# Maxima of the scores as quads beside the wide products, and unit sums shared between POOL and VectorE

## What is computed

```
def _qdq(x):                       # int8 fake quantisation of the last axis
    s = jnp.maximum(jnp.max(jnp.abs(x), axis=-1, keepdims=True) / 127.0, 1e-08)
    return jnp.clip(jnp.round(x / s), -127.0, 127.0) * s
# attention; x here is layernorm(x)
q = _qdq(x) @ _qdq(wq).T + bq
kv = cond @ wkv.T + bkv
attn = jax.nn.softmax(jnp.einsum('bnhd,bmhd->bhnm', q, k) * scale, axis=-1)
o = jnp.einsum('bhnm,bmhd->bnhd', attn, v).reshape(B, N, C)
out = _qdq(o) @ _qdq(wp).T + bp
# layer
x = x + tanh(g_xattn) * attention(layernorm(x), ctx)
h = layernorm(x)
x = x + tanh(g_ffn) * ((silu((h @ f8(gate_w)) * gate_scale) * ((h @ f8(up_w)) * up_scale)) @ f8(down_w)) * down_scale
```

## Time and profile before

| | us |
|---|---|
| median of 3 runs | 1103.12 (1101.31 to 1110.62) |
| the profiled execution, its own time | 1105.23 |
| its span, first to last instruction | 1103.5 |
| TensorE busy | 967.0 (88%) |
| VectorE busy | 706.6 (64%) |
| POOL busy | 457.2 (41%) |
| ScalarE busy | 446.8 (40%) |
| mean granted TensorE clock | 0.957 of full speed |

### The profile page before, as it was taken

The page is one execution under the profiler, slowest core; times in us unless marked ns, Lnnn a source line. Parts: engine busy times, 40 slices in busy tenths (PEclk is TensorE's granted clock), DMA queues, the critical chain, the costliest instruction groups (busy, mean ns, idle before and its releaser), DMA issues.

```text
span 1103.5 us, 15274 instructions
## 1 busy us (share of the span) xinstructions
PE 967.0 (88%) x5192; PEld 328.0 (30%) x5192; DVE 706.6 (64%) x985; ACT 446.8 (40%) x793; POOL 457.2 (41%) x416
## 2 busy tenths in 40 slices
PE   4476899998999899988999789989899979985698
PEld 1231111234443212224443212214443312212343
DVE  6879899447638756468557757665666856654522
ACT  4330365642340266662341156673232146674130
POOL 3335788860410288940220088860130066630130
PEclk9698799999999999999999989999999989997799
DMA  7244242220002412010001322001001231000001
GB/s 257 72 117 112 58 120 70 75 87 1 1 18 62 111 55 52 13 57 1 1 7 39 105 79 63 20 20 39 1 1 43 72 91 44 1 1 0 1 1 39
DMA packets 34289, 55.41 MB, mean 50 GB/s; under 512 B 8416, under 2 KB 14624, under 8 KB 34208
## 3 DMA queue, kind: packets, MB, share of 16 engines
q1 hardware_dynamic: 29280, 38.58, 12.1%
q0 software_dynamic: 4800, 15.73, 4.9%
q10 hardware_dynamic: 128, 0.07, 0.0%
HBM read 31.21 MB, written 4.19 MB: 32 GB/s over the span
## 4 chain that ended last, share of the span: by engine, by line
issue 34%; PE 33%; POOL 14%; DVE 11%; ACT 4%; DMA 3%; POOLq 0%; ACTq 0%; DVEq 0%
PE ps L1095 10%; PE ps L1159 7%; PE ps L1148 6%; PE ps L1173 4%; PE ps L1135 3%; POOL acc L498 2%; ACT r L680 2%; DVE mx L906 2%; POOL r L569 2%; PE ps L1386 2%; POOL ctx_hi L469 2%; POOL ctx_lo L473 1%; DMA cf<-in_ctxT 1%; POOL w_down L501 1%; POOL w_up L501 1%
## 5 line engine op out<-in xcount | busy, mean ns | idle before, releaser
L906 DVE TENSOR_REDUCE mx<-ps 128x2 f32<-128x1024 f32 x256 | 306.9, 1220 | 113.5 <-PE ps L1135 107.0
L680 ACT ACTIVATE r<-ps 128x512 f32<-128x512 f32 x512 | 279.7, 595 | 208.3 <-PE ps L1148 189.7
L1148 PE MATMUL ps<-qst,kst 97*128 97x512 f16 x512 | 168.9, 394 | 35.5 <-ACT r L680 25.3
L552 POOL TENSOR_TENSOR acc<-r,acc 128x512 f32<-128x512 f32 x108 | 134.5, 1280 | 16.1 <-ACT r L680 15.3
L1159 PE MATMUL ps<-r,vv 128*32 128x512 f32 x1024 | 140.3, 621 | 0.0
L1135 PE MATMUL ps<-k_reg,q_reg 32*128 32x512 f16 x512 | 102.8, 401 | 17.0 <-DVE mx L906 16.7
L569 POOL TENSOR_TENSOR r<-q_reg,r 128x512 f16<-128x512 f32 x48 | 57.0, 1188 | 142.2 <-ACT r L705 142.2
L522 POOL TENSOR_TENSOR xres<-xres,bp_bc 128x512 f32<-128x512 f32 x16 | 19.7, 1267 | 193.4 <-DMA xres<-in_x 193.3
L1095 PE MATMUL ps<-k_reg,w_gate 128*128 128x512 f16 x384 | 90.7, 379 | 7.2 <-DVE k_reg L1021 7.2
L1031 DVE SCALAR_TENSOR_TENSOR q_reg<-ps,us_c,q_reg 128x512 f32<-128x512 f32 x48 | 35.9, 749 | 88.4 <-PE ps L1095 87.9
L1095 PE MATMUL ps<-k_reg,w_up 128*128 128x512 f16 x384 | 90.7, 379 | 0.0
(11 more groups left out here) (139 smaller groups left out, 1226.0 us busy)
## 6 DMA issues: line engine op xcount, KB each, us to landing
kst<-k_reg SPq DMA_DIRECT2D x192, 64.0 KB, 2.0
qst<-q_reg SPq DMA_DIRECT2D x192, 32.0 KB, 1.9
cf<-in_ctxT POOLq DMA_DIRECT2D x24, 256.0 KB, 3.4
qst<-in_x SPq DMA_DIRECT2D x4, 1024.0 KB, 5.1
xres<-in_x SPq DMA_DIRECT2D x4, 1024.0 KB, 6.2
acc<-in_gate_w POOLq DMA_DIRECT2D x12, 256.0 KB, 3.3
acc<-in_up_w POOLq DMA_DIRECT2D x12, 256.0 KB, 3.0
acc<-in_down_w POOLq DMA_DIRECT2D x12, 256.0 KB, 2.9
```

What stands on the lines that cost most here:

```text
L552: nc.gpsimd.tensor_tensor(acc[:, j, :], prob[:, i % P_SLOTS, :], other, ALU.add).then_inc(p_pool, 1)
L680: nc.scalar.activation(prob[:, i % P_SLOTS, :], bank(S_RING[i % 2]), ACT.Exp, scale=SCALE).then_inc(exp_done, 1)
L906: nc.vector.tensor_reduce(mx[:, g % 2, t, half, 2 * pair:2 * pair + 2], ps[:, M_PAIRS[p % 2]:M_PAIRS[p % 2] + 2, :], AX.X, ALU.max).then_i ...
L1148: nc.tensor.matmul(bank(S_RING[i % 2]), kst[0:97, SLOTS[g], j, t * P:(t + 1) * P], qst[0:97, SLOTS[g], j, :], start=True, stop=True).then_ ...
```

## The change

All four batches are written out in Python; no hardware loop is left. The parts:

- **Order between units.** SX and XT of the next batch stand in the chain ahead of X2T; then come, as one run of wide products `WIDE`, Q0 to Q3, K0 to K7, GU0 to GU23, DOWN0 to DOWN3, in banks 0 to 3 by turns. x of the next batch is normalised and quantised by VectorE during the units (`x_ahead`, at `AHEAD_UNITS`) and not during the gates.
- **Maxima as quads.** A quad computes all four heads of a group at once, in banks 4 to 7, and VectorE reduces it in two instructions of 128x1024. 24 quads (groups 0 to 2) stand between or inside the wide products: one in each of K2 to K7, one behind each gate (a shift step takes one place), two in each DOWN. Group 3's 16 pairs stay in the units, one to a unit, in banks 6 and 7 alone.
- **Batch 0** has group 0 and half of group 1 as quads beside V and ahead of the units, the rest as pairs, two steps at the end of each of units 0 to 20, all in banks 6 and 7.
- **Units.** Two heads' scores go to banks 0, 1, two to banks 2, 3; one exponential takes two banks (128x1024). `values` and `sums` follow the four scores. Sums have bank 5, values bank 4.
- **Additions.** For batches 1 to 3, units 0 to 5 of every group are added: heads 0 and 1 by POOL, heads 2 and 3 by VectorE. Units 6 and 7 stay with TensorE.
- **POOL.** The context of batch b + 2 is split during the gates (three chunks) and DOWN (five) of batch b, and not during units. The residual's bias follows the additions.
- **SP.** k and q are stacked in two slots instead of three. The shift row moves from ScalarE's queue to SP's, behind the group's 24 DMAs. The output is stored by tile in every batch.
- **Memory.** x, its integers, o's transposes and others have tiles of their own or other ones to share.

```diff
-A_RING = (0, 1, 7, 6)
-S_RING = (0, 1)
-M_PAIRS = (2, 4)
-O_BANK, DEN_BANK = 6, 7
+FREE_RING, HEAD_RING, V_RING = (0, 1, 2, 3), (0, 1, 4, 5), (0, 1)
+O_BANK, DEN_BANK, QUAD, PAIR = 4, 5, 4, 6
...
+CHAIN = (["V0"] + CHAIN_LAST[0:5] + ["V1", "V2", "V3"] + CHAIN_LAST[5:9] + ["V4"] + CHAIN_LAST[9:13]
+         + ["V5", "V6", "V7"] + TURNED + CHAIN_LAST[13:])
+WIDE = HI_SEQ + FFN_SEQ
...
+STEPS0 = {"V2": quads(0, 0, 1), "V3": quads(0, 1, 2), "V4": quads(0, 2, 3), "V5": quads(0, 3, 4),
+          "V6": quads(0, 4, 6), "V7": quads(0, 6, 8)}
+LEAD0 = quads(1, 0, 1) + [("S", 0, 0)] + quads(1, 1, 4)
+UNIT_LIST0 = (pairs(1, 8) + pairs(2, 0, 1) + [("S", 1, 0)] + pairs(2, 1) + pairs(3, 0, 1) + [("S", 2, 0)]
+              + pairs(3, 1) + [("S", 3, 0)])
+UNIT_STEPS0 = {u: UNIT_LIST0[2 * u:2 * u + 2] for u in range(G * MT)}
+K_STEPS = {f"K{n}": [s] for n, s in zip(range(2, 8), quads(0, 0, 6))}
+GU_LIST = quads(0, 6, 8) + quads(1, 0, 1) + [("S", 0, 0)] + quads(1, 1) + quads(2, 0, 1)
+DOWN_LIST = [("S", 1, 0)] + quads(2, 1)
+UNIT_STEPS = {u: [s] for u, s in enumerate([("S", 2, 0)] + pairs(3), 1)}
+AHEAD_UNITS = ((2, 4, 6) + tuple(range(16, 32)), (2, 3, 4) + tuple(range(9, 24)))
...
-ADDED, ADDED_LAST = (0, 2, 4, 6), (0, 1, 2, 3, 4, 5)
+ADDED = (0, 1, 2, 3, 4, 5)
+CHUNKS_BY_GATES = (3, 6, 9)
...
 POOL
+                    for j in range(2):
+                        i = u * HG + j
+                        pool.wait_ge(exp_done, pair_count(b, u, j))
...
+                        nc.gpsimd.tensor_tensor(acc[:, j, :], prob[:, i % P_SLOTS, :], other,
+                                                ALU.add).then_inc(p_pool, 1)
...
 ScalarE
+                    for j in range(0, HG, 2):
+                        if u >= 2 and added(b, u - 2):
+                            act.wait_ge(p_pool if j == 0 else p_dve, adds_count(b, u - 2, j + 1))
+                        s = (u * HG + j) % P_SLOTS
+                        act.wait_ge(s_full, pair_count(b, u, j))
+                        nc.scalar.activation(prob[:, s:s + 2, :], ps[:, j:j + 2, :], ACT.Exp,
+                                             scale=SCALE).then_inc(exp_done, 1)
...
 VectorE
+                    if kind == "Q":
+                        t, half = divmod(i, 2)
+                        for k in range(2):
+                            nc.vector.tensor_reduce(mx[:, g % 2, t, half, 2 * k:2 * k + 2],
+                                                    ps[:, QUAD + 2 * k:QUAD + 2 * k + 2, :], AX.X,
+                                                    ALU.max).then_inc(m_free, 1)
...
+                    maxima(b, (UNIT_STEPS if b else UNIT_STEPS0).get(u, []))
+                    if not last and u in AHEAD_UNITS[b > 0]:
+                        next(ahead, None)
+                    if added(b, u):
...
+                        for j in range(2, HG):
...
+                                nc.vector.tensor_tensor(acc[:, j, :], acc[:, j, :], prob[:, i % P_SLOTS, :],
+                                                        ALU.add).then_inc(p_dve, 1)
...
 TensorE
+            def maxima(b, s):
+                kind, g, i = s
+                before = PREVIOUS[b, s]
...
+                else:
+                    pe.wait_ge(m_free, FREE_BEFORE[b, s])
...
+                if kind == "Q":
+                    t, half = divmod(i, 2)
+                    heads, first_bank = range(HG), QUAD
+                else:
+                    t, half, k = i // 4, i // 2 % 2, i % 2
+                    heads, first_bank = range(2 * k, 2 * k + 2), PAIR
+                for k, j in enumerate(heads):
+                    rows = slice(j * DH, (j + 1) * DH)
+                    mm = nc.tensor.matmul(bank(first_bank + k), qhi[rows, g, t * P:(t + 1) * P],
+                                          khi[rows, g, half * 512:(half + 1) * 512], start=True, stop=True)
+                mm.then_inc(m_full, 1)
+            def scores(b, u, j):
...
+                if u > 0:
+                    pe.wait_ge(exp_done, pair_count(b, u - 1, j))
...
+                for k in range(2):
+                    mm = nc.tensor.matmul(bank(j + k), kst[0:97, g % 2, j + k, t * P:(t + 1) * P],
+                                          qst[0:97, g % 2, j + k, :], start=True, stop=True)
+                mm.then_inc(s_full, 1)
...
+            for b in range(B):
+                for u in range(UNITS):
+                    scores(b, u, 0)
+                    scores(b, u, 2)
+                    if u >= 1:
+                        values(b, u - 1)
+                        sums(b, u - 1)
+                    if b > 0 and t == 0 and g > 0:
+                        totals(b, g - 1)
+                    for s in (UNIT_STEPS if b else UNIT_STEPS0).get(u, []):
+                        maxima(b, s)
```

More of the change, by code:

```diff
@@ L186, in pairs_done, with d_seq, d_full_count, d_free_count @@
-def pairs_done(p):
-    return sum(s[0] == "P" for s in STREAM[:p + 1])
-def added(first, u):
+def d_seq(b):
+    return D_SEQ_LAST if b == B - 1 else D_SEQ
+def d_full_count(b, name):
+    return b * len(D_SEQ) + d_seq(b).index(name) + 1
+def d_free_count(b, name):
+    seq = d_seq(b)
+    return b * D_FREES + sum(map(by_dve, seq[:seq.index(name) + 1]))
+def d_bank(b, name):
+    return (D_BANK_LAST if b == B - 1 else D_BANK)[name]
+def d_before(b, name):
+    seq = d_seq(b)
+    same = [n for n in seq[:seq.index(name)] if d_bank(b, n) == d_bank(b, name)]
+    return same[-1] if same else None
@@ L570, in body @@
                                             ALU.subtract).then_inc(f_ready, 1)
-                    if i == 1 and not last:
-                        inverse_deviation(b * 2 + 3)
-            batches(pool, body)
+                    if ahead and i in CHUNKS_BY_GATES:
+                        chunk(b + 2, CHUNKS_BY_GATES.index(i))
+                for c in range(len(CHUNKS_BY_GATES), CHUNKS if ahead else 0):
+                    chunk(b + 2, c)
         @block.scalar
@@ new lines, in q_product, with scales_product, turn_x @@
+            def q_product(out, n, full):
+                pair(out, [(wqT[:, k, n * P:(n + 1) * P], xqT[:, k, :]) for k in range(CT)], full)
+            def scales_product(out, full):
+                for t in range(NT):
+                    mm = nc.tensor.matmul(out[:, t * P:(t + 1) * P], onesf[:, :],
+                                          diag[:, t * P:(t + 1) * P], start=True, stop=True)
+                mm.then_inc(full, 1)
+            def turn_x(out_bank, n, full):
+                turn(bank(out_bank, dt=BF16), [xq[:, t, n * P:(n + 1) * P] for t in range(NT)], full)
@@ L1282, in body @@
+            for s in LEAD0:
+                maxima(0, s)
+            pe.wait_ge(rows_set, 1 + G)
+            for b in range(B):
+                last = b == B - 1
                 for u in range(UNITS):
                     g, t = divmod(u, MT)
-                    behind_values, behind_sums = unit_steps(g, t)
-                    score(b, u, 0)
-                    score(b, u, 1)
+                    scores(b, u, 0)
+                    scores(b, u, 2)
                     if u >= 1:
-                        values(b, u - 1, first)
@@ new lines, in _ @@
+                for name in d_seq(b):
+                    out_bank = d_bank(b, name)
+                    out = bank(out_bank)
+                    kind = name.rstrip("0123456789") if name[:3] != "X2T" else "X2T"
+                    n = int(name[len(kind):] or 0)
+                    ahead = [lambda s=s: maxima(b + 1, s) for s in AHEAD.get(name, [])] if not last else []
+                    before = d_before(b, name)
+                    if before is None:
+                        pass
+                    elif before[:2] == "GU":
@@ L1388, in body @@
                         mm.then_inc(d_full, 1)
-                        for p in ahead:
-                            maxima(b + 1, False, p)
-            batches(pe, body)
 def kernel(**inputs):
```

1106 lines of the change are left out of this document (511 added, 595 removed).

## The result

The changed kernel takes 1113.96 us in the median of 10 runs (1108.87 to 1117.11), the kernel before 1101.65 in runs beside it (1098.82 to 1110.62): ratio 1.0104, 95% interval 1.0077 to 1.0131. The forecast was 1078 us, within 1046 to 1112; the measured time lies 2 us above that range and 36 above the forecast. The profiled execution took 1109.91 us, its span is 1108.1. This execution lies 4 us under its kernel's median, that of before 3.6 over its own, so the two traces show 4.6 us of difference where the runs show 12.

A forecast was written before the change was run, and what follows sets the result against it. TensorE's queue order was taken as the bound: exponentials wait for late scores, pairs come only after the gates. Terms +4 +24 -21 -9 -8 -17 = -27 took the span from 1103.5 to 1076.5; with 1.7 around it, 1078 us, range 1046 to 1112.

The forecast's parts named there:

- Start: Ahead of the first exponential, 24 reduces instead of 22 and two banks for V instead of four: +4 us, bounds 0 and +8.
- quads: Four matmuls on four row groups, unseen before: taken as 0.33 us, bounds 0.32 and 0.64.
- FFN stretches: Batches 0 to 2, FFN plus the next batch's Q, K and maxima: 100.2 us each, together -21, bounds -30 and -8.
- batch 0's units: Two maxima steps at a unit's end, the second waiting for the first's reduce: 140 us against 116.0, +24, bounds +15 and +45.
- The 7 us added for clock and VectorE: In batch 0's units: +4 for VectorE's work exceeding its free time in about eight units, +3 for a lower clock.
- Chains ... keep their work: 0, and whatever slips there counts in full.: Chains and last FFN keep their work: 0 us; any slip there counts in full, since nothing covers it.
- 5.5 us of them in added units: Batches 1 and 2: preparing the next x takes turns with POOL, 5.5 us of it in added units, bounds 0 and 11.
- Added units, 3.45 us: Batches 1 to 3, units 0 to 5 of each group: both engines' additions take turns, 3.45 us a unit, bounds 2.5 and 3.9.
- (a): Rival, no collision: VectorE's addition runs beside POOL's, units fall to 2.5 us, time 1035 us; chance 0.1.
- (b): Rival, slower by the clock in batch 0's units: 8.5 us a unit at 1.2 GHz, time 1114 to 1153 us; chance 0.15.
- (c): Rival, nothing moves: four-head maxima at 0.64 us (+13) and added units at 3.9 (+20), time 1111 us; chance 0.2.

## Why the prediction was wrong

Of the 31.6 us by which the traced span exceeds the forecast, 10.8 are the rest of batch 0, 12.1 the units of batches 1 and 2, and 3.9 those of batch 3.

- **Start, quads, FFN stretches, batch 0's units**: right, within 2 us each. The largest loss (+24, measured +26) and the largest gain (-21) were priced from rows. (The FFN terms as printed add up to 99.2 and not 99.4, which changes nothing.) In batch 0's units the sum is better than its parts: at 4.9 and 2.9 us a unit groups 0 to 3 come to some 38, 39, 33 and 23, measured were 46.3, 40.2, 33.8 and 21.7. The 7 us added for clock and VectorE turned up nearly all in group 0, whose clock was 0.79. In the five other kernels with the same units that group took 43.2 or 43.3.
- **"Chains ... keep their work: 0, and whatever slips there counts in full."** This step failed, with 10.8 us. The rule in it was right and was not applied: VectorE's magnitudes slipped there. I had counted them as VectorE's time within batch 0's units and checked POOL's 96 us against the stretch, but not the order of `W_UNITS`, which leaves 8 of 26 magnitudes to the last 8 units. Those units run at 2.7 us, while the magnitudes there start 3.1 to 4.0 us apart, all but the first behind a load, and three of them came after the last exponential. The magnitudes early took the stretch to 136.3. In batches 1 and 2 the chain slipped by 1.8 us each (36.9 for 35.1), which was not followed up.
- **Units of batches 1 and 2, "5.5 us of them in added units"**: this term failed too, the units by 7.5 and 4.6 us. I costed the preparation of x as time taken in turns; what it costs is its place, ahead of additions on which an exponential two units on waits. The same work, placed from unit 6 on in the summed units only, gave 8.3 and 6.9 us back.
- **Added units, 3.45 us**: right, 3.43. The group around five of them, from POOL's first addition to the next group's, was 25.9 to 26.4 us and not 25: three groups, 3.2 of batch 3's 3.9. Most of it lies where from unit 7's exponentials to the next group's first addition pass 4.35 us and not 3.6 (932.38 less 928.03). This is read from the trace alone.
- **The rivals.** (a) is refuted by the 3.43 us. (b) gave its sign, a granted clock under 0.9, in batch 0's group 0 (0.79) and in batch 1's units (0.89), where TensorE waited. It did not decide batch 0 as (b) has it: over all its units the clock was 0.92, and they met the forecast. The mean granted clock went from 0.957 to 0.935 and rose to 0.961 in the kernel with x moved. What part of the time is the clock's own was not separated from the waits beside it. (c), at 1111, is near in time by luck: quads cost 0.33 and an added unit 3.43. Its sum is also short, since a batch has 20 such units and not 15, so the rival as described costs 27 us and not 20.
- **What was not asked.** The working priced the turns and then set them against the old units of 3.6 us, not against units without any additions on the new frame. With the sums kept, TensorE needs 1.0 + 1.0 + 0.9 + 0.32 = 3.2 us a unit, less than 3.45; measured were 95.6 / 32 = 3.0.

## What to carry to other kernels

Before giving work to a second engine, price the unit without the offload: here the engine to be relieved needed less than the two helpers in turns, while one helper alone, in five units of eight, still paid. Where queues run in order, check what stands in them when a stretch ends: a backlog moves into the chain behind, where nothing covers it. And where two steps share a buffer, set other products between them.

## What the runs showed of the hardware

When additions of VectorE (two SBUF inputs) and POOL meet, one of each takes 1.70 us (ten in 17.00, five in 8.50), where VectorE's alone starts every 0.60: each POOL instruction costs VectorE 1.1 us, a little less than its own 1.29. The Trainium skill, "SBUF — State Buffer", section SBUF: two separate sides, calls the shared ports an exclusive lock, held for an instruction; ten of each in nearly the same time agree with it. Whole lengths added up, 0.68 + 1.29 = 1.97 us, would be too long by 0.27. The reduce, which reads PSUM, keeps its 1.21 us beside POOL's additions. Also stretched are copies with one input: two took 2.35 us together, where one takes 0.42 in the kernel whose additions are VectorE's alone.
